# Layer 0 of a two-layer kernel: the order of VectorE's work per batch element, key projection an element ahead, residuals summed in PSUM

## What is computed

```python
h = layernorm(x) * (1 + ca) + sa
xs = shift(h, by one token)
k, v, r = (h*m + xs*(1-m)) @ W.T          # one mix m and one W for each of the three
# scan over the tokens, wn = -exp(w):
#   y = (e1*aa + e2*v) / (e1*bb + e2), p = max(pp, u + k), pp' = max(pp + wn, k)
x = x + ga * ((sigmoid(r) * y) @ Wo.T)
h = layernorm(x) * (1 + cb) + sb
x = x + gb * (quantise(h) @ quantise(W).T + bias)   # blocks of 32, FP6 grid
```

## Time and profile before

| | us |
|---|---|
| median of 3 runs | 1836.62 |
| lowest and highest | 1834.87, 1838.26 |
| the profiled execution | 1837.68 |
| its span in the profile | 1835.9 |
| TensorE busy | 1707.4 (93%) |
| ScalarE busy | 1215.9 (66%) |
| VectorE busy | 1162.3 (63%) |
| GpSimd busy | 679.4 (37%) |
| layer 0 with setup, to the first custom instruction of layer 1 | 229.62 |

### The profile page before, as it was taken

One profiled execution on the slowest core, in us unless ns is written; L12 is line 12 of the kernel. 1 busy time (PEld: TensorE's weight loads), 2 busy tenths in 40 slices (PEclk: granted clock), 3 DMA queues, 4 the chain that ended last, 5 costly groups with the idle time before them and its releaser, 6 DMA issues.

```text
span 1835.9 us, 33808 instructions
## 1 busy us (share of the span) xinstructions
PE 1707.4 (93%) x10588; PEld 1063.3 (58%) x10588; DVE 1162.3 (63%) x3679; ACT 1215.9 (66%) x3383; POOL 679.4 (37%) x697
## 2 busy tenths in 40 slices
PE   5676689999999999999999999999999999999998
PEld 3433446665666656665666556665666566656664
DVE  5999666656656666655665656566665666565675
ACT  2564367757776767676676777676767777677773
POOL 0456533443333333334344433333333334343300
PEclk8787699999999999999999999999999999999999
DMA  4001021112111211222111211121122211121101
GB/s 173 1 0 26 16 67 41 41 33 58 37 41 37 50 47 41 53 45 53 41 41 36 63 32 42 37 49 44 41 53 46 53 41 41 42 61 32 41 17 46
DMA packets 71295, 80.91 MB, mean 44 GB/s; under 512 B 29520, under 2 KB 37840, under 8 KB 70992
## 3 DMA queue, kind: packets, MB, share of 16 engines
q1 hardware_dynamic: 71120, 78.76, 17.4%
HBM read 7.91 MB, written 2.10 MB: 5 GB/s over the span
## 4 chain that ended last, share of the span: by engine, by line
PE 72%; DVE 9%; ACT 9%; issue 7%; POOL 2%; DMA 0%; SPq 0%; DVEq 0%; POOLq 0%; ACTq 0%
PE bank L1862 24%; PE bank L1883 13%; PE bank L1826 8%; PE bank L1716 4%; PE bank L1717 3%; ACT arena L1002 2%; PE bank L1774 2%; PE bank L1712 2%; PE bank L1780 2%; PE bank L1789 2%; DVE arena L1452 1%; PE bank L1836 1%; ACT arena L994 1%; PE bank L1671 1%; PE bank L1770 1%
## 5 line engine op out<-in xcount | busy, mean ns | idle before, releaser
L1452 DVE CUSTOM_DVE_ANT_0 arena<-bank,W 128x512 f32<-128x512 f32 (+3 forms) x1024 | 478.6, 487 | 464.0 <-PE bank L1862 434.5
L1002 ACT ACTIVATE arena<-arena 128x512 f32<-128x512 f32 (+3 forms) x1024 | 569.9, 557 | 304.8 <-DVE arena L1452 300.0
L1862 PE MATMUL bank<-arena 96*128 96x512 f32 (+3 forms) x2048 | 696.6, 442 | 0.0
L1862 PEld LDWEIGHTS bank<-arena 96*128 96x128 f32 x2048 | 350.7, 192 | 191.6 <-issue 124.8
L1883 PE MATMUL bank<-W,arena 128*128 128x128 f32 x2560 | 418.3, 277 | 9.0 <-ACT arena L1002 7.1
L1883 PEld LDWEIGHTS bank<-W,arena 128*128 128x128 f32 x2560 | 307.2, 141 | 176.2 <-issue 98.7
L994 ACT ACTIVATE arena<-bank 128x512 f32<-128x512 f32 (+1 forms) x512 | 277.0, 541 | 124.1 <-PE bank L1883 120.3
L739 POOL TENSOR_TENSOR arena<-arena,one 128x512 f32<-128x512 f32 x64 | 66.5, 1039 | 708.0 <-DVE arena L1420 533.2
L1002 ACT ACTIVATION_READ_ACCUMULATOR arena<-arena 128x1 f32 x1024 | 195.3, 191 | 0.0
L1463 DVE COPY arena<-bank 128x384 f32<-128x384 f32 x256 | 141.7, 554 | 72.5 <-PE bank L1883 72.5
L1826 PE MATMUL bank<-arena 128*32 128x256 f32 (+1 forms) x3072 | 165.7, 349 | 0.0
(11 more groups left out here) (255 smaller groups left out, 2076.3 us busy)
## 6 DMA issues: line engine op xcount, KB each, us to landing
arena<-arena SPq DMA_DIRECT2D x896, 64.0 KB, 2.0
arena<-arena SPq DMA_DIRECT2D x64, 128.0 KB, 2.4
W<-wide SPq DMA_DIRECT2D x1, 3730.0 KB, 13.3
X<-x SPq DMA_DIRECT2D x8, 256.0 KB, 5.9
out<-arena SPq DMA_DIRECT2D x8, 256.0 KB, 2.3
arena<-arena SPq DMA_DIRECT2D x96, 16.0 KB, 1.8
LW<-lat SPq DMA_DIRECT2D x1, 768.5 KB, 14.3
arena<-mods SPq DMA_DIRECT2D x1, 768.0 KB, 4.9
```

Of the source, the lines that this page charges most:

```text
L1002: done = A(here, here, ACT.Exp, bias=nmax[:, c:c + 1], scale=-1.0, accum_out=lsum[:, c:c + 1])
L1452: last = v.tensor_tensor_reduce(Pb[:, s % 4, at_p:at_p + n], bank[turn.score_bank(s)][:, at:at + n], w("mask", T - n), -1.0, 3e38, ALU.add ...
L1862: last = MM(B_[:, at:at + n], query(t), Kb[a][g % 2][0:QD, h, 0:n], start=True, stop=True)
```

## The change

On VectorE, `wkv` is cut in three. `summed(b)` ends with the denominators, and its first scan now stands behind the two products that read the values' bank; `maxima(b+1)` follows, then `inverse(b)` (the reciprocal), `quantised_ffn(b-1)`, `weighted(b)`. The moments of the input run three elements ahead instead of two and stand in front of those of x1. Both residual adds leave VectorE: TensorE adds X or x1 to bank[4] or bank[6] by a product with the identity, and ScalarE copies the bank to x1 or X. On TensorE the key projection runs an element ahead, behind that element's transposes; value and receptance projection open the turn. ScalarE has a new order. In the setup, the first element's moments and their deviation come ahead of the wait for the modulation, and `rows(0)` goes from the front of TensorE's loop to turn -1. GpSimd makes the input deviation three elements ahead.

```diff
@@ gpsimd
+            deviation(0, 0, s_var1, mva, s_z, s_dev1)
             pool.wait_ge(s_setup, 1)
...
-                if 0 <= b + 2 < B:
-                    deviation(b + 2, 0, s_var1, mva, s_z, s_dev1)
+                if b == -1:
+                    deviation(1, 0, s_var1, mva, s_z, s_dev1)
+                if 1 < b + 3 < B:
+                    deviation(b + 3, 0, s_var1, mva, s_z, s_dev1)
@@ scalar
             def exponentials(b):
                 act.wait_ge(s_qd, b + 1)
                 if b > 0:
-                    act.wait_ge(s_rw, b)
+                    act.wait_ge(s_den, b)
...
+            def keep_ffn(b):
+                act.wait_ge(s_y, b + 1)
+                if b > 1:
+                    act.wait_ge(s_ffn, b - 1)
+                A(x1[:, b % 2].rearrange("p a c -> p (a c)"), bank[4][:], ACT.Copy).then_inc(s_x1, 1)
+
+            def keep_attention(b):
+                act.wait_ge(s_ffn, b + 1)
+                A(X[:, b * T:(b + 1) * T], bank[6][:], ACT.Copy).then_inc(s_x2, 1)
...
+            normed_mix(0)
             act.wait_ge(s_setup, 1)
-            row_read(0)
             for b in range(-2, B + 1):
-                if 0 <= b + 1 < B:
-                    normed_mix(b + 1)
-                    mix_input(b + 1)
+                if b == -1:
+                    exponentials(0)
+                    row_read(0)
+                if 0 < b + 2 < B:
+                    normed_mix(b + 2)
+                if 0 <= b - 2 < B:
+                    normed_attention(b - 2)
+                if 0 <= b + 2 < B:
+                    mix_input(b + 2)
                 if 0 < b < B:
                     row_read(b)
...
                 if 0 <= b - 2 < B:
-                    normed_attention(b - 2)
                     attention_input(b - 2)
+                if 0 < b + 1 < B:
+                    exponentials(b + 1)
                 if 0 <= b + 1 < B:
                     receptance(b + 1)
                 slot(b, "mid")
+                if 0 <= b < B:
+                    keep_ffn(b)
                 if 0 <= b - 1 < B:
                     ffn_input(b - 1)
-                if 0 <= b + 1 < B:
-                    exponentials(b + 1)
                 slot(b, "out")
+                if 0 <= b - 1 < B:
+                    keep_attention(b - 1)
                 if 0 <= b < B:
                     normed_ffn(b)
@@ vector
             step(TS(wn, nwn, -1.0, None, ALU.mult))
+            norm_mix(0)
             v.wait_ge(s_modc, 1)
...
             def norm_ffn(b):
-                v.wait_ge(s_y, b + 1)
-                kept = x1[:, b % 2]
-                step(TT(kept.rearrange("p a c -> p (a c)"), X[:, b * T:(b + 1) * T], bank[4][:], ALU.add))
-                step.settle()
-                moments(lambda j: kept[:, j], st6b, mvb).then_inc(s_var2, 1)
+                v.wait_ge(s_x1, b + 1)
+                moments(lambda j: x1[:, b % 2, j], st6b, mvb).then_inc(s_var2, 1)
...
             def norm_attention(b):
-                v.wait_ge(s_ffn, b + 1)
-                step(TT(X[:, b * T:(b + 1) * T], x1[:, b % 2].rearrange("p a c -> p (a c)"), bank[6][:], ALU.add))
-                step.settle()
+                v.wait_ge(s_x2, b + 1)
                 moments(lambda j: tile(b, j), st6, mv).then_inc(s_var3, 1)
...
                 if 0 <= b < B:
-                    wkv(b)
+                    summed(b)
+                if 0 <= b + 1 < B:
+                    maxima(b + 1)
+                if 0 <= b < B:
+                    inverse(b)
+                if 0 <= b - 1 < B:
+                    quantised_ffn(b - 1)
+                if 0 <= b < B:
+                    weighted(b)
...
-                if 0 <= b - 1 < B:
-                    quantised_ffn(b - 1)
-                if 0 <= b + 1 < B:
-                    maxima(b + 1)
                 if b == 0:
                     latent_weights()
+                if b == -1:
+                    norm_mix(1)
+                if 1 < b + 3 < B:
+                    norm_mix(b + 3)
                 if 0 <= b < B:
                     norm_ffn(b)
                 if 0 <= b - 2 < B:
                     keep_moments(b - 2)
-                if 0 <= b + 2 < B:
-                    norm_mix(b + 2)
@@ tensor
             def project_out(b):
+                pe.wait_ge(s_rowsa, b + 1)
+                MM(bank[4][:], ident, X[:, b * T:(b + 1) * T], start=True, stop=False)
                 pe.wait_ge(s_rw, b + 1)
...
             def ffn(b):
...
+                pe.wait_ge(s_x1, b + 1)
+                MM(bank[6][:], ident, x1[:, b % 2].rearrange("p a c -> p (a c)"), start=False, stop=False)
                 pe.wait_ge(s_xdTr, b + 1)
...
-            rows(0)
             for b in range(-2, B + 1):
...
                 if 0 <= b + 1 < B:
-                    turn_input(b + 1)
-                    project_mixes(b + 1)
+                    project_value(b + 1)
+                    project_receptance(b + 1)
+                if b == -1:
+                    rows(0)
+                if 0 <= b + 2 < B:
+                    turn_input(b + 2)
                 if 0 <= b - 2 < B:
                     turn_attention(b - 2)
+                if 0 <= b + 2 < B:
+                    project_key(b + 2)
                 slot(b, "mid")
                 if 0 <= b < B:
                     project_out(b)
```

More of the change, by code:

```diff
@@ L438, in build @@
         s_den = sem("denominator_summed")
+        s_x1 = sem("x1_kept")
+        s_x2 = sem("x2_kept")
         s_arg = sem("exponents_ready")
@@ L1149, in gate_fix, with tile, norm_mix @@
                 step(STT(x, ta, -1.0, tb, ALU.add, ALU.mult))
+            def tile(b, j):
+                return X[:, ds(b * T + j * P, P)]
+            def norm_mix(b):
+                if b == 0:
+                    v.wait_ge(s_x0, 16)
+                if b == 1:
+                    v.wait_ge(s_x, 16 * (B - 1))
+                if b > 0:
+                    v.wait_ge(s_dev1, b)
+                moments(lambda j: tile(b, j), st6a, mva).then_inc(s_var1, 1)
             v.wait_ge(s_tc, 1)
@@ L1226, in wkv, with inverse, weighted @@
                 TT(den, den, ex[:, 0], ALU.add).then_inc(s_den, 1)
-                step.settle()
+            def inverse(b):
                 v.wait_ge(s_den, b + 1)
                 step(v.reciprocal(den, den))
+            def weighted(b):
                 step.settle()
@@ L1569, in _ @@
             step.settle()
+            v.wait_ge(s_x2, B)
             v.wait_ge(s_h3, B - 1)
@@ L1677, in project_out @@
                 for j in range(NT):
-                    last = MM(bank[4][:, j * P:(j + 1) * P], rw[:, j * P:(j + 1) * P], wog, start=True, stop=True)
+                    last = MM(bank[4][:, j * P:(j + 1) * P], rw[:, j * P:(j + 1) * P], wog, start=False, stop=(j == NT - 1))
                 last.then_inc(s_y, 1)
```

47 lines of the change are left out of this document (25 added, 22 removed).

## The result

The changed kernel takes 1844.1 us (median of 5 runs, 1842.31 to 1845.87) against 1836.62 before: ratio 1.0036, 95% interval 1.0024 to 1.0049. By the medians it is 7.5 us slower, a ratio of 1.0041, inside the interval; the ratio given is worth 6.6. The forecast was +2.5 us; the result lies inside the range, on the slow side of it.

What follows compares the result with a forecast made beforehand. VectorE was taken to bound layer 0, with the change exposing a trip through TensorE and ScalarE. The terms -3.7 + 4.35 + 3.3 - 3.7 + 2.3 gave +2.5 us: 1839 us, range 1828 to 1848.

Steps and rivals of the forecast that it cites:

- What bounds the loop: Layer 0: VectorE is the bound, busy 19.32 of 20.38 us per element; change removes 1.4 us of adds, exposes a trip.
- trip: From weighted values through TensorE and ScalarE to the output moments: 5.13 us at full clock, 8.8 at half, 6.6 taken.
- The signs that the forecast named: VectorE idle 2 to 5 us ahead of output moments in elements 1-5; projection near 1.9 us; sums at 26.8, 47.4.
- Setup: Up to second sums: first sums 6.1 us earlier, much given back in element 0; 3.7 us gained, bounds 0 to 6.1.
- Elements 1 to 4: Four elements at 22.4 us each, 89.6 instead of 85.25: +4.35 us, bounds -1.7 to +12.95.
- Work up to the weighted values: VectorE per element, from sums to weighted values: 14.55 us instead of 11.07, with maxima 1.86 and quantising 1.82 in front.
- Element 5: 25.3 us instead of 21.99, with a reader fill and GpSimd's shared key: +3.3 us, bounds +1.8 to +5.4.
- Element 6: Waits of 1.42 and 1.37 and 1.4 of adds go, rotation costs 0.8 more: -3.7 us, bounds -4.5 to -2.
- Element 7 and the end: Trip exposed twice from element 7's sums to the end of layer 0: +2.3 us taken.
- The one before: In element 7's stretch, first of two exposed trips, ahead of the last one: -0.3 to +1.4 us.
- Half clock all through: Rival: everything in the trip at half clock, 8.8 us; total +14, 1851 us; chance 0.12.
- Late ScalarE: Rival: exponentials and tanh ahead of x1 copy make ScalarE late, 1 to 3 us in five elements; 1847 us; chance 0.12.

Runs made afterwards that it cites:

- decode_late: Changed kernel with GpSimd's decoding of b-1 made to wait for the weighted values of b; 1839.7 us, ratio to before 1.0010.
- ffn_first: Changed kernel with FFN part of b-1 ahead of b's projection, input moments and reciprocal reordered around weighting, last-turn reads as in tail; 1834.85 us, ratio to before 0.9976.
- tail: Changed kernel with ScalarE's layer-1 reads ahead of the norm of element 6's output in the last turn; 1843.63 us, ratio to before 1.0034.
- adds_back: Changed kernel with both residual adds back on VectorE, without identity products and ScalarE copies; 1845.09 us, ratio to before 1.0041.
- ffn_first2: ffn_first with element 3's ScalarE read behind the residual copy, GpSimd's shared key and query rope behind the decoding; 1832.46 us, ratio to before 0.9963.

## Why the prediction came out as it did

**What bounds the loop: right.** The forecast said that the change takes 1.4 us of adds off VectorE and exposes a trip through TensorE and ScalarE worth more. VectorE's busy time fell, the stretch grew, ScalarE's copies end both waits. With the decoding out of the way (decode_late) elements 1 to 4 still take 86.88 against 85.25, and making the trip run earlier as well (ffn_first, 80.19) turned the sign. The signs that the forecast named came only in part: a wait of 2 to 5 us ahead of the output moments was there in two of five elements (1.77, 3.04, 0.92, 1.64 and 4.05), and so was the projection at half clock.

**Setup: right.** 26.8 and 47.4 forecast for the first and second sums, 26.71 and 46.97 measured. The exponentials no longer stand behind the tanh, and element 0 gives part back.

**Elements 1 to 4: nearly the right sum from two wrong terms.** The forecast of an element was 14.55 + 6.6 + 1.2 = 22.4, the measured mean 15.22 + 5.69 + 1.20 = 22.1. "Work up to the weighted values" was counted from VectorE's rows alone. The quantising was moved ahead of the weighting, and with it went the moment at which GpSimd begins to decode: now beside an instruction with two inputs, which takes 1.42 instead of 0.69. The step that failed is the sum of durations taken from rows where nothing ran beside them. The prediction did count such a price for the shared key in element 5, and did not ask the same of the decoding. The trip was 6.6 in the forecast because one burst was taken for all. It is 4.93 at full clock (5.13 forecast), 7.25 at half clock in element 2. In element 3, 0.73 us of the 5.66 is ScalarE's read for layer 1, which the prediction put into "idle time that VectorE and ScalarE now have". The tanh (L878) that must precede it waits for the weighted values, so this idle time lies ahead of it and can't be used.

**Element 5: nearly right** (25.3 forecast, 25.53 measured), again from terms that are off against each other: 16.07 us to the weighted values (16.55 forecast with the 2.0 for the shared key), and a trip of 8.26 at half clock that includes the fill (7.5 forecast). **Element 6:** the wait for the rank read went as forecast; 0.9 us of the gain did not come. decode_late has the same 31.36, so it isn't the decoding. The timeline shows what it is, GpSimd's rotation (170.78 to 179.11) beside VectorE's instructions with two inputs:

```profile
174.91 1.57 DVE L1262 TENSOR_TENSOR arena<-arena 128x512 f32<-128x512 f32 x1
```

The two beside it took 1.53 (L1135) and 1.64 (L1267); undisturbed each takes 0.69, so they cost 2.7 us more in all. Before the change the rotation met one of them (1.47, 0.8 more). The forecast added 0.8 for it, and it was 1.9.

**Element 7 and the end: the step that made the difference,** +6.99 instead of +2.3. "The one before costs -0.3 to +1.4" was +2.94. Before the change, VectorE reaches this trip 11.07 us after the sums, and quantising (1.8) is done inside it. After, it reaches it after 13.5 (1.8 of quantising and 0.73 of the decoding's contention in front), and the trip itself is no shorter (8.39 against 7.91). In elements 1 to 5 the prediction counted the quantising into the sum; here it priced the trip alone. The last trip was +1.39, within its +0.8 to +1.7. And 2.53 us more came from a queue that the prediction did not walk: ScalarE's new order put the norm of element 6's output ahead of the layer-1 reads, and TensorE's fill waits for such a read. tail removes that and the stretch falls by 2.73.

**The total.** Against the forecast the five stretches are off by -0.4, -1.1, +0.2, +0.9 and +4.7 us, 4.3 in all. That the total fell inside the range is owed to the range's width of 20 us as much as to the terms.

**The rivals.** Half clock all through would have made the trip 8.8 us; no element from 1 to 4 came to it (7.25 at most). The rule of the Trainium skill, "TensorE: Matmul & The Clock Gate" (HAM oscillation), that waits between bursts throttle TensorE anew in every round agrees with adds_back, where every projection from element 1 on is at half clock, and not with the changed kernel, where three of the five in elements 1 to 5 are at full clock. Late ScalarE was given for another reason (exponentials ahead of the x1 copy): in elements 1, 2 and 4 the copy ran within 0.05 us of the projection's end. It came true in element 3 and in the last turn, through reads for layer 1.

## What to carry to other kernels

When a step is moved on one engine, write down what each consumer of it now runs beside, and look up what that neighbour costs: here the helper on GpSimd started 0.6 us ahead of the instruction that the whole loop waits for and doubled it. Walk every in-order queue through the irregular turns too, the first, the last and those with guests: 2.5 us of the 4.7 by which that term was missed were in the last turn. In this kernel, taking work from the busiest engine paid when what its successor needs is made under a long instruction (the FFN part under the reciprocal), not when it is started after it.

## What the runs showed of the hardware that was not expected

The length of an idle time alone does not tell the granted clock behind it. The kernel before ran at full clock (1.00 from 124.0 to 127.4), idled 2.58 us and came back at half clock (130.10); the changed one came back at full clock after 2.80 us (element 3, clock 1.00) and at half clock after 4.17 (element 2). Two more projections at half clock followed short idle times, 0.70 us (element 7) and 1.43 us (adds_back, element 1), but there the clock had been at 0.50 before the idle time began. TensorE's product just ahead of the 0.70 us:

```profile
203.31 1.92 PE L1720 MATMUL bank<-X,W 128*128 128x512 f32 x2
```

The same code behind layer 0 took 1602.3 to 1609.2 us in ten profiled executions, although none of the edits touches it. And 3.3 us were lost in ffn_first2 in two elements whose code is the same, at a lower clock. So a gain of 2 us in a profile (tail) may not be seen in the total, and an edit's effect is better read from its own stretch. No edit is needed for such a spread: 15 executions of the kernel before on one chip ran from 1834.47 to 1840.22. Whether the timing at which layer 1 starts adds to it was not tried.

GpSimd and VectorE together: 1.43 and 1.42 us beside each other, 1.05 and 0.69 one after the other. Overlap in the timeline was no overlap in work.
